# Recommendation tower on one core: a new order of the work per block of samples, gathers a product step later, first ids spread by the tensor engine

## The reference

```python
e = jnp.stack([tbl_0[ids[:, 0]], ..., tbl_25[ids[:, 25]]], axis=1)      # (2048, 26, 128)
combined = jnp.concatenate([dense[:, None, :], e], axis=1)
inter = jnp.einsum('bfd,bgd->bfg', combined, combined)[:, TRIU_I, TRIU_J]   # 351 pairs
h = jnp.concatenate([dense, inter, dense], axis=1)                       # 607
h = jnp.maximum(h @ W_top1 + b_top1, 0.0)                                # 512
h = jnp.maximum(h @ W_top2 + b_top2, 0.0)                                # 256
y = h @ W_top3                                                           # (2048, 1)
```

## Time and profile before

| what | value |
|---|---|
| median of 3 runs | 520.17 us (515.14 to 522.7) |
| profiled execution | 515.3 us, span 513.2 us |
| PE busy | 408.8 us (80%), weight loads 365.9 us |
| DVE, ACT, POOL busy | 262.7, 208.7, 254.1 us |
| PE's mean granted clock | 0.88 of full |
| DMA | 36.34 MB, mean 71 GB/s |

### The profile page before, as it was taken

The page is one execution under the profiler, slowest core; times in us unless marked ns, Lnnn a source line. Parts: engine busy times, 40 slices in busy tenths (PEclk is TensorE's granted clock), DMA queues, the critical chain, the costliest instruction groups (busy, mean ns, idle before and its releaser), DMA issues.

```text
span 513.2 us, 14192 instructions
## 1 busy us (share of the span) xinstructions
PE 408.8 (80%) x6280; PEld 365.9 (71%) x6280; DVE 262.7 (51%) x323; ACT 208.7 (41%) x436; POOL 254.1 (50%) x265
## 2 busy tenths in 40 slices
PE   5886727777978598875978788887989689789977
PEld 4776716767878497764967687785878588778755
DVE  3789505654555554663553655655364655454220
ACT  3456302234343543444342553435243543337432
POOL 5778875551555555552555535553555535540000
PEclk8998857776999898988897978997898969899989
DMA  6994251230322222221222212221232212210000
GB/s 170 227 240 107 67 158 50 70 108 23 74 59 78 56 64 68 69 64 32 64 66 70 63 49 64 67 74 49 68 68 69 63 42 70 58 39 1 4 1 0
DMA packets 27972, 36.34 MB, mean 71 GB/s; under 512 B 9151, under 2 KB 21959, under 8 KB 27912
## 3 DMA queue, kind: packets, MB, share of 16 engines
q1 hardware_dynamic: 19704, 18.65, 14.6%
q0 software_dynamic: 8192, 16.79, 13.5%
q10 hardware_dynamic: 16, 0.01, 0.0%
HBM read 35.42 MB, written 0.01 MB: 69 GB/s over the span
## 4 chain that ended last, share of the span: by engine, by line
PE 71%; issue 13%; ACT 4%; SPq 4%; DMA 4%; DVE 2%; another core or an unknown queue 1%; ACTq 0%; DVEq 0%
PE ring L411 17%; PE ring L412 15%; PE gram L449 10%; PE ring L485 8%; PE ring L431 7%; PE ring L494 6%; DMA dense<-in_r_dense_features 4%; PE ring L483 3%; SPq L281 2%; PE ring L461 2%; PE ring L472 2%; DVE pairs_and_more L674 2%; PE ring L503 2%; ACT pairs_and_more L578 1%; SPq L275 1%
## 5 line engine op out<-in xcount | busy, mean ns | idle before, releaser
L359 POOL DMA_INDIRECT rows<-in_tbl,ids_all x256 | 248.7, 971 | 201.1 <-PE gram L449 127.3
L651 DVE TENSOR_TENSOR onehot<-idb,vrow 125x1024 fp32r<-125x1024 f32 x160 | 192.7, 1222 | 130.5 <-PE ring L412 58.7
L411 PE MATMUL ring<-onehot,table_hi 125*128 125x256 f32 x608 | 181.6, 328 | 22.1 <-DVE pairs_and_more L674 7.6
L412 PE MATMUL ring<-onehot,table_lo 125*128 125x256 f32 x608 | 169.5, 309 | 0.0
L411 PEld LDWEIGHTS ring<-onehot,table_hi 125*128 125x128 f32 x608 | 132.9, 219 | 28.8 <-issue 8.7
L412 PEld LDWEIGHTS ring<-onehot,table_lo 125*128 125x128 f32 x608 | 133.4, 219 | 0.8
L559 ACT COPY xt<-ring 128x256 f32<-128x256 f32 x80 | 54.2, 677 | 128.9 <-PE ring L412 68.3
L449 PE MATMUL gram<-xt 128*27 128x26 f32 x4096 | 55.1, 201 | 42.6 <-issue 40.0
L449 PEld LDWEIGHTS gram<-xt 128*27 128x27 f32 x4096 | 47.8, 114 | 51.7 <-issue 46.0
L567 ACT COPY xt<-ring 128x512 f32<-128x512 f32 (+1 forms) x56 | 51.2, 987 | 24.1 <-remote 16.0
L431 PE MATMUL ring<-ident,rows 128*128 128x128 f32 x256 | 38.6, 285 | 13.6 <-issue 6.7
(11 more groups left out here) (41 smaller groups left out, 209.7 us busy)
## 6 DMA issues: line engine op xcount, KB each, us to landing
ids_spread<-in_ids_t SPq DMA_DIRECT2D x70, 128.0 KB
rows<-in_tbl,ids_all POOLq DMA_INDIRECT x256
xt<-in_tbl SPq DMA_DIRECT2D x6, 448.0 KB
w<-in_tbl SPq DMA_DIRECT2D x3, 448.0 KB
rows<-in_ids_t SPq DMA_DIRECT2D x10, 128.0 KB, 5.7
dense<-in_r_dense_features SPq DMA_DIRECT2D x16, 64.0 KB
w<-in_W_top SPq DMA_DIRECT2D x4, 256.0 KB
w<-in_W_top SPq DMA_DIRECT2D x1, 512.0 KB
```

The lines of the kernel that those rows point to most:

```text
L359: pool.indirect_dma_start(rows[:, i % ROWS, :], None, aps[f"tbl_{f}"], bass.IndirectOffsetOnAxis(ap=ids_all[:, k, f:f + 1].bitcast(U32), a ...
L411: pe.matmul(ps, table_hi[:, m, c * KC + k, :], chosen, start=first, stop=False)
L412: last = pe.matmul(ps, table_lo[:, m, c * KC + k, :], chosen, start=False, stop=final)
L651: dve.tensor_tensor(onehot[:, (CH * u + c) % SLOTS], idb[0:VP, u % 2, 0:BS].unsqueeze(1).to_broadcast([VP, KC, BS]), vrow[:, c * KC:(c + 1 ...
```

## The change

The list of stages is written anew. Per block n in the steady state, before and after (L = lookup of block n+1 unless marked, U = unblock, R = rows, P = pairs):

| behind step | before | after |
|---|---|---|
| (n, 0) | L0, layer1 0 of n-1, L1, layer1 1, L2 | U0 U1 of n-1, L3, U2 U3, layer3 of n-2, R(n,1) 0 1, L4, L5 |
| (n, 1) | R(n,1) 0 1, layer1 2, L3, R 2 3, layer1 3, R 4, L4 | P0 P1 of n-1, L6, R(n,1) 2 3 4, layer1 0 of n-1, L7 |
| (n, 2) | L5, layer2 0 of n-1, L6, layer2 1, L7, layer3 | layer1 1 of n-1, R(n+1,0) 0 1, L8, L9 |
| (n, 3) | L8, U0 U1 of n, R(n+1,0) 0 1, U2 U3, R 2 3 4, L9, P0 P1 P2 | layer2 0 of n-1, R(n+1,0) 2 3 4, L0 of n+2, layer2 1, L1 L2 of n+2 |

A layer1 or pairs stage now fills a bank with two blocks. The copies of the products have a stage of their own in the list (`grams`), which PE passes over, and change engines: DVE has the even steps, ACT the odd ones. The gathers wait for one product step more, and POOL's two subtractions stand ahead of the fourth group. The ids of the first block come by one DMA of 10 x 256 values, and PE spreads them over the partitions by a product with a column of the identity (`spread_first_ids`). `ROWS` and the three one-hot slots are as they were; the one-hot chunks are made one chunk further ahead.

```diff
-        yield from lookups(0, *range(NL - 2))
-        yield from rows(0, 0, 0, 1)
-        yield from lookups(0, NL - 2)
-        yield from rows(0, 0, 2, 3, 4)
+        yield "first_ids", 0, 0, 0
+        yield "first_ids", 0, 1, 0
+        for m in range(NL - 1):
+            if m + 2 < NL:
+                yield "first_ids", 0, m + 2, 0
+            yield from lookups(0, m)
+        yield from rows(0, 0, 0, 1, 2, 3, 4)
         yield from lookups(0, NL - 1)
         for n in range(NB):
             yield "products", n, 0, 0
-            yield from lookups(n + 1, 0)
+            yield from layer("unblock", n - 1, 0, 1)
+            yield from lookups(n + 1, *([0, 1, 2] if n == 0 else [3]))
+            yield from layer("unblock", n - 1, 2, 3)
+            yield "grams", n, 0, 0
+            yield from layer("layer3", n - 2, 0)
+            yield from rows(n, 1, 0, 1)
+            yield from lookups(n + 1, *([3] if n == 0 else [4, 5]))
...
-        return g == 1 or (t, g) == (1, 3)
+        return t == 1 and g in (1, 3)
...
-    FIRST_GROUPS_BEHIND = {1: 0, 2: 3, 3: 6, 4: 9}
+    FIRST_GROUPS_BEHIND = {1: 0, 2: 3, 3: 6}
...
+            sp.dma_start(first_ids_i, aps["ids_t"][:, 0:BS]).then_inc(first_ids_landed, 16)
             sp.dma_start(ids_all[:], ids.rearrange("(t p) f -> p t f", p=P)).then_inc(ids_landed, 16)
             for m in range(NL):
-                spread_ids(m)
                 load_raw(m)
-            load_dense(0)
-            load_dense(1)
+                if m in (3, 6):
+                    load_dense(m // 4)
...
-                    pool.wait_ge(gram_ready, group - 4)
+                    pool.wait_ge(gram_ready, group - 3)
...
+                    if (k, g) == (1, GROUP):
+                        for m in LO_ON_GPSIMD:
+                            lower_part(m)
                     if g % GROUP == 0:
                         wait_for_turn(i // GROUP)
-                    u, first = divmod(i - IDS0, IDS_ROWS)
-                    if 0 <= u < NL and first == 0:
-
-                        pool.wait_ge(idb_ready, u + 1)
...
+            def spread_first_ids(m):
+                if m == 0:
+
+                    pe.wait_ge(first_ids_ready, 1)
+                if m >= 2:
+
+                    pe.wait_ge(onehot_ready, CH * (m - 1))
+                pe.matmul(idb[0:VP, m % 2, 0:BS], ident[0:NL, m:m + 1].to_broadcast([NL, VP]), first_ids, start=True,
+                          stop=True).then_inc(first_idb_ready, 1)
...
-                    pe.wait_ge(gram_act if s % 2 == 0 else gram_dve, step // 2)
+                    pe.wait_ge(gram_dve if s % 2 == 0 else gram_act, step // 2)
...
+            one_hot(1, 0)
             for stage, n, a, b in stages():
                 if stage == "lookup":
                     u = n * NL + a + 1
...
                     if u < NB * NL:
-                        one_hot(u, 0)
...
                         one_hot(u, 1)
+                    if u + 1 < NB * NL:
+                        one_hot(u + 1, 0)
```

More of the change, by code:

```diff
@@ L91, in stages @@
+            yield from layer("pairs", n - 1, 0, 1)
+            yield from lookups(n + 1, *([4, 5] if n == 0 else [6]))
+            yield from rows(n, 1, 2, 3, 4)
             yield from layer("layer1", n - 1, 0)
-            yield from lookups(n + 1, 1)
+            yield from lookups(n + 1, *([6] if n == 0 else [7]))
+            yield "products", n, 2, 0
+            yield "grams", n, 2, 0
             yield from layer("layer1", n - 1, 1)
-            yield from lookups(n + 1, 2)
-            yield "products", n, 1, 0
@@ L97, in stages @@
-            if n == 0:
-                yield from lookups(n + 1, 3)
-            yield from rows(n, 1, 0, 1)
-            yield from layer("layer1", n - 1, 2)
-            if n > 0:
-                yield from lookups(n + 1, 3)
-            yield from rows(n, 1, 2, 3)
-            yield from layer("layer1", n - 1, 3)
-            yield from rows(n, 1, 4)
-            yield from lookups(n + 1, 4)
-            if n == NB - 1:
-                yield from layer("layer2", n - 1, 0)
-            yield "products", n, 2, 0
@@ L124, in stages @@
-            yield from layer("unblock", n, 0, 1)
-            yield from rows(n + 1, 0, 0, 1)
-            yield from layer("unblock", n, 2, 3)
-            yield from rows(n + 1, 0, 2, 3, 4)
-            yield from lookups(n + 1, 9)
-            yield from layer("pairs", n, 0, 1, 2)
-        yield from layer("layer1", NB - 1, 0, 1, 2, 3)
+            yield from lookups(n + 1, *([7] if n == 0 else []))
+            yield from rows(n + 1, 0, 0, 1)
+            yield from lookups(n + 1, 8, 9)
+            yield "products", n, 3, 0
@@ new lines, in stages @@
+            yield "grams", n, 3, 0
+            yield from layer("layer2", n - 1, 0)
+            yield from rows(n + 1, 0, 2, 3, 4)
+            yield from lookups(n + 2, 0)
+            if n == NB - 1:
+                yield from layer("unblock", n, 0, 1)
+            yield from layer("layer2", n - 1, 1)
+            yield from lookups(n + 2, 1, 2)
+        yield from layer("unblock", NB - 1, 2, 3)
+        yield from layer("layer3", NB - 2, 0)
+        yield from layer("pairs", NB - 1, 0, 1)
@@ L131, in stages @@
+        yield from layer("layer1", NB - 1, 0, 1)
         yield from layer("layer2", NB - 1, 0, 1)
@@ L616, in _ @@
                     store_rows(n, a, b)
-                elif stage == "products" and a % 2 == 0:
+                elif stage == "grams" and a % 2 == 1:
                     store_products(n, a)
```

138 lines of the change are left out of this document (67 added, 71 removed).

## The result

| what | before | after |
|---|---|---|
| median of 20 runs | 519.5 us (513.7 to 527.2) | 514.6 us (505.5 to 521.1) |
| ratio of the two | | 0.986, 95% interval 0.9815 to 0.9905 |
| profiled execution, its span | 515.3, 513.2 us | 505.5, 503.7 us |
| PE's mean granted clock | 0.88 | 0.91 |

The account below looks back on a forecast made before the run. The prediction took the rhythm of gather groups and product steps as the bound, with late signals behind step 3. Start 66, 26 intervals x 13.0 = 338, then 12.9, 43.5 and 2.1 made 462.5 us; range 449 to 487.

Parts of the forecast that it names:

- The floor is the gather group's: Between product steps: eight gathers hold PE's product step until 1.6 us after the last, so no interval goes below 12.87 us.
- Signals are late from some 6 us into the group, one per 1.45 us: In a gather group's second half, others see PE's completions late; earlier signals take 0.3 us.
- the term of 13.0 us per interval: Steady state, group 5 to group 31: 26 intervals between group starts at 13.0 us each, 338 us.
- All four walks end before the release: PE's work, timed from group start, ends at 11.0, 9.6, 8.4 and 11.0 us behind steps 0 to 3; release at 11.4.
- Rows group 1 of the first half moves to ACT: Smaller edit: 1.2 us per block goes from DVE to ACT, both at or below half busy; cost 0.
- Starved lookups and the clock: Rival: lookups at each quarter's end wait for chunks, PE's clock drops, 4.6 us in every interval; 578 us, chance 0.06.
- The stall moves along: Rival: unblock's stores and late chunks still stall, mean interval stays 14.65 us; 505 us, chance 0.08.
- PE-bound, no floor: Rival: intervals come down to PE's own work, 11.6 us a quarter; 426 us, chance 0.06.
- The start: Up to group 5's start, paced by POOL's gathers: put at 66 us, with 62 to 69 as its limits.
- Gathers a step later, cost in steady state 0: Group g waits for step g-4, not g-5; a group takes 9.7 us, within one interval, so cost 0.
- The end: From group 31's start: 12.9 us to the end of step (7,0), then 43.5 us, where the tail was 41.45.
- The range: Stated as 449 to 487 us with chance 0.80; its own terms gave 446 and 492 us.

Follow-up runs that it names:

- k_gate5: Changed kernel with the gathers' old gate (group g waits for product step g-5): 520.5 us, ratio 0.998 to the kernel before (522.0 us).
- m_held: Changed kernel, ten memsets behind each gather group; ACT and DVE take rows groups 0 and 1 behind step 0 only after them: 500.05 us.
- n_held_act: Changed kernel with ten memsets per gather group, the same rows groups held, and the copy of rows group 1 on ACT: 478.1 us.
- h_floor_after: Changed kernel with five POOL memsets behind each gather group, for which a product step waits: 456.9 us, kernel before 405.8 us.
- after_copy: Changed kernel run again unchanged, on the quick kind of machine: 398.0 us, ratio 0.981 to the kernel before.
- e_rows_act: Changed kernel with the copy of rows group 1 of the second tile on ACT, not DVE: 398.9 us, ratio 0.983 to the kernel before.
- f_spread: Changed kernel with all four unblock banks first behind step 0 and the list behind step 3 reordered: 398.6 us, ratio 0.984 to the kernel before.

## Why the prediction was wrong

*The floor is the gather group's: right.* Intervals behind step 1 at 12.8 to 13.2, and the two pairs above. The prediction had inferred it from time alone; one of these pairs stood in the trace of before already, behind (6,3), unused.

*Signals are late from some 6 us into the group, one per 1.45 us: the step that failed.* The step of 1.45 us is in the new trace too (1.43), but the walk gave each interval only one or two signals that are late by that much: "lookup 4 half seen near 8.8, chunk at 10.0", lookup 5 over at 11.0 and ready before the release. In the trace unblock 2 is late already in the fourth microsecond, rows 0 and 1 wait until 11.4, the chunk is ready at 13.7, and the term of 13.0 us per interval measured 14.54, 40.2 us in all.

What sets the length of the delay is not shown. By the list, PE sends 14 signals behind step 0 (two per lookup, one per other bank, one for the step), 11, 8 and 12 behind steps 1 to 3; before it was 9, 12, 10 and 17, so that a block has 45 for 48. The blocks shown fit a rule by number (17.8, 13.1, 12.8, 15.5 us; and 13.1, 13.9, 12.9, 17.5), but others don't: 10 signals took 14.0 to 14.3 us behind step 2 in three blocks of the kernel before, and 12 took from 13.8 us behind its step 1 to 17.4 behind step 3 of k_gate5. So the number is not all, and the run that would vary it never fell on the slow kind.

*All four walks end before the release: wrong behind steps 0 and 3*, right behind 1 and, in most blocks, 2. m_held and n_held_act show for step 0 that a late rows copy ahead of lookup 5's chunk on DVE is enough, and h_floor_after that without late signals the order keeps a floor in nearly all intervals. For step 3 the account is read from the trace alone. "Rows group 1 of the first half moves to ACT" was costed at 0; the copy of group 1 of the second half, left on DVE, costs 3 to 4 us a block where it alone is late (500.05 against 478.1 us).

*Starved lookups and the clock.* The rival had this mechanism and 6%, but in all four intervals. It came true in two, though the clock did not always follow. Behind step 0 PE idles for 3.3 us inside lookup 5, and the clock from there to the end of the interval is 0.50 to 0.63 in five of the six blocks, 1.00 in the sixth. Behind step 3 it is 0.63 to 1.00 over the last 4.6 us. I had put the chunk waits at 1.5 us. The Trainium skill (TensorE: Matmul & The Clock Gate, HAM oscillation) has the array back at half clock after idle gaps between bursts; the trace agrees over 302.60 to 306.62 (0.50), and so does m_held over 298.99 to 302.82 (0.55), behind its held signals. *The stall moves along* is the rival that happened: 505 us, against a profiled 505.5, a match that is in part luck, for its start is 5 us too early and its end 2 us too late. I gave it 8%, though my own walk was within 0.4 us of the release in two places.

*PE-bound, no floor*: wrong for the slow kind, and what the quick kind does.

*The start*: group 5 was put at 66 us and came at 71.1. "In gather count this is no gain" was right or worse: group 6 starts at 84.3, before at 80.1. Counted by product steps it is a gain of 9 us, since one group fewer runs before step (0,1). *Gathers a step later, cost in steady state 0*: right in the steady state, but by k_gate5 it was the part with most of the gain. *The end*: 12.4 and 42.0 us for 12.9 and 43.5, right. *The range*: its own terms came to 446 and 492 us, and 449 to 487 was stated; neither reaches 514.6.

## What to carry to other kernels

When signals are seen late in a trace, do not carry over the lateness of the one or two that it shows: a new order puts other signals into the same stretch, and here they came up to 7 us late. Then look at what is queued behind the reader on the same engine. Before calling a floor a floor, look for the one interval in the same trace that lacks the suspected cause: here it was behind (6,3), and it told at once what gathers cost. A reordered list can move a stall and leave its size.

## What the runs showed of the hardware

The same kernel takes 405 us on some machines and 520 us on others. The single instructions are as long: gathers 959 and 971 ns, one-hot chunks 1219 and 1222 ns. The bytes are the same. What differs is the time from PE's end of work to the others' start beside gathers (lookup 4 of after_copy is over at 236.66 and taken at 236.69; rows 0 of the changed kernel is over at 293.6 and taken at 300.27), the interval from one product step to the next beside eight gathers (12.8 us and more in the steady state, against 10.1 to 11.6), and, with PE's idle time, its clock (0.99 and 0.88). Why the two kinds differ stays open. Open too is what e_rows_act and f_spread do on the slow kind, for both ran on the quick kind alone. From the trace I expect e_rows_act to gain little there, not the 3 us a block of the held runs: the chunk can't start before its own signal, and if signals arrive in the order in which PE gives them, that is not before rows 1 is taken, so at most the copy's 1.2 us a block.
